# Expert rows scaled at the expert tile and summed in memory by adding DMAs, on one Trainium2 core

## What is computed

```python
def layer(x, w_qkv, b_qkv, w_out, b_out, w12, w3, gate_w):   # cut to what matters
    xn = layernorm(x)
    qkv = xn @ w_qkv + b_qkv                                 # windows of 128, stride 64, 16 heads
    attn = (softmax(q @ k.T / sqrt(16)) @ v)[:, :512] @ w_out + b_out
    top, idx = top_k(xn @ gate_w.T, 2)
    p = softmax(top)
    h = silu(xn @ w1[e]) * (xn @ w2[e])                      # for both experts e of a token
    ffn = sum(p[k] * (h[k] @ w3[idx[k]].T) for k in (0, 1))
    return x + attn + ffn
```

## Time and profile before

| | |
|---|---|
| median of 3 runs | 704.5 us (704.3 to 704.83) |
| the profiled execution: own time, span | 704.97 us, 703.2 us |
| mean granted TensorE clock | 0.981 |
| busy: TensorE, VectorE, ScalarE, GpSimd | 90%, 81%, 73%, 40% of the span |
| DMA | 92.62 MB, mean 132 GB/s |
| the chain that ended last, by engine | PE 65%, DVE 14%, ACT 10%, issue 7% |

### The profile page before, as it was taken

How to read it: one execution, slowest core, us unless ns; L and a number is a source line. 1 busy time by engine, 2 the same in 40 slices (tenths; PEclk the granted TensorE clock), 3 DMA queues, 4 the chain that set the end, 5 groups by cost and what they waited for, 6 DMA issues and landing times.

```text
span 703.2 us, 17940 instructions
## 1 busy us (share of the span) xinstructions
PE 630.0 (90%) x5914; PEld 509.7 (72%) x5915; DVE 567.5 (81%) x902; ACT 513.2 (73%) x882; POOL 281.5 (40%) x330
## 2 busy tenths in 40 slices
PE   0786785989999999999999999999999999999985
PEld 0554564765888888888888888888767676666663
DVE  4968899986888888888888888888587979788884
ACT  4554578396787787777877877777577788888885
POOL 3000274033344444444544544444201336666654
PEclk9998789899999999999999999999999999999999
DMA  9795478491111111111111111111178778885740
GB/s 299 263 257 193 110 251 305 121 314 48 53 52 52 60 52 52 59 48 57 53 52 60 52 53 60 52 52 54 38 192 242 180 246 209 262 228 159 207 141 31
DMA packets 66337, 92.62 MB, mean 132 GB/s; under 512 B 6432, under 2 KB 53408, under 8 KB 66272
## 3 DMA queue, kind: packets, MB, share of 16 engines
q1 hardware_dynamic: 57904, 70.56, 33.8%
q0 software_dynamic: 6816, 18.62, 7.9%
q10 hardware_dynamic: 1568, 2.76, 1.2%
HBM read 58.93 MB, written 32.83 MB: 130 GB/s over the span
## 4 chain that ended last, share of the span: by engine, by line
PE 65%; DVE 14%; ACT 10%; issue 7%; POOL 2%; DMA 1%; ACTq 0%; DVEq 0%; POOLq 0%
PE PS L1319 57%; PE PS L1570 4%; DVE SMALL L980 4%; ACT WORK L785 3%; PE PS L1548 2%; DVE XN L1138 2%; DVE WALL L974 2%; ACT QS L780 1%; DMA XN<-in_x 1%; DVE WORK L1049 1%; DVE WORK L1042 1%; ACT WORK L723 1%; DVE WALL L998 1%; ACT SIDE L792 1%; POOL OTS L595 1%
## 5 line engine op out<-in xcount | busy, mean ns | idle before, releaser
L367 DVE TENSOR_TENSOR WS<-WALL,WS 128x1024 fp32r<-128x1024 f32 x134 | 164.4, 1227 | 55.2 <-ACT WS L877 40.8
L1319 PE MATMUL PS<-WS,XTS 128*128 128x512 f32 x804 | 203.9, 402 | 0.0
L1319 PEld LDWEIGHTS PS<-WS,XTS 128*128 128x128 f32 x804 | 146.2, 189 | 30.5
L877 ACT ACTIVATE WS<-WALL 128x1024 fp32r x134 | 141.6, 1056 | 8.8 <-issue 0.3
L1319 PE MATMUL PS<-DOWN_HIGH,HTS 128*128 x568 | 115.9, 289 | 0.8 <-ACT HTS L892 0.8
L595 POOL TENSOR_TENSOR OTS<-SIDE,XN 128x256 f32<-128x256 f32 x30 | 22.8, 761 | 205.2 <-DVE XN L1138 138.5
L1319 PEld LDWEIGHTS PS<-DOWN_HIGH,HTS 128*128 128x128 f32 x568 | 90.9, 188 | 1.6 <-issue 1.5
L980 DVE TENSOR_REDUCE SMALL<-PS 128x8 f32<-128x1024 f32 x64 | 77.5, 1211 | 12.2 <-PE PS L1319 11.9
L785 ACT ACTIVATE WORK<-PS 128x512 f32<-128x512 f32 x128 | 69.4, 595 | 23.6 <-PE PS L1319 20.3
L667 POOL DMA_INDIRECT ys_scratch<-SIDE,SIDX x36 | 43.8, 1218 | 93.2 <-ACT SIDE L908 93.2
L663 POOL DMA_INDIRECT XS<-xn_scratch,GIDX x71 | 71.8, 1011 | 23.0 <-issue 21.3
(11 more groups left out here) (147 smaller groups left out, 1090.9 us busy)
## 6 DMA issues: line engine op xcount, KB each, us to landing
WALL<-in_wexp SPq DMA_DIRECT2D x28, 384.0 KB, 7.1
WALL<-ys_scratch SPq DMA_DIRECT2D x16, 512.0 KB, 7.2
parts_scratch<-WORK SPq DMA_DIRECT2D x32, 240.0 KB, 2.4
QS<-parts_scratch SPq DMA_DIRECT2D x16, 480.0 KB, 4.6
XN<-in_x SPq DMA_DIRECT2D x4, 1024.0 KB, 12.1
xn_scratch<-XN SPq DMA_DIRECT2D x4, 1024.0 KB, 7.3
WALL<-in_x SPq DMA_DIRECT2D x8, 512.0 KB, 5.9
KS<-parts_scratch SPq DMA_DIRECT2D x16, 240.0 KB, 4.1
```

The source lines that it names most:

```text
L367: eng.tensor_tensor(out=WS[:, 1 - k, half, 1], in0=weights, in1=WS[:, 1 - k, half, 0].bitcast(F32), op=ALU.subtract).then_inc(low_ready[ha ...
L877: act.activation(WS[:, 1 - k, half, 0], weights, ACT.Copy).then_inc(high_ready[half], 1)
L1319: return pe.matmul(o, a, b, start=start, stop=stop)
```

## The change

The rows of `xn_scratch` get two elements more: the share of the token's first choice and the difference of the second's to it. ScalarE stores them at batch 0, unit 5. A gather brings them along; GpSimd makes of them and of `KIND` (1 in slots of second choices) the share of each slot (`find_share`), and ScalarE's copy of a tile's result scales by it. `sum_scratch` replaces `ys_scratch`: one row for a token. SP copies `x` into it, GpSimd adds the attention rows of batches 0 and 1 (`keep`), and each scatter adds its rows, one scatter after the other. Behind the stage, `rest` loads one tensor, `own` is one add and is made for batches 2 to 7, `later`, `scale` and `combine` are gone, and batches 0 and 1 are copied from `sum_scratch` to the output.

```diff
-DUMP_ROW = 2 * B * L
+DUMP_ROW = B * L
+ROW = D + 2
...
-        XS = sb("XS", [P, 2, D])
+        XS = sb("XS", [P, 2, ROW])
...
-            yv = ys_dram[0:DUMP_ROW].rearrange("(k t p) d -> p t k d", k=2, p=P)
+            def copy_x(b):
+                r = slice(b * L, (b + 1) * L)
+                sp.dma_start(sum_dram[r], x[r]).then_inc(x_copied[b], 16)
 
             def rest(b):
-
                 t = slice(b * TB, (b + 1) * TB)
-                sp.dma_start(XR[:, t, :], xv[:, t, :]).then_inc(rest_in[b], 16)
-                for k in range(2):
-                    sp.dma_start(YG[:, t, k, :], yv[:, t, k, :]).then_inc(rest_in[b], 16)
...
+                sp.dma_start(XR[:, t, :], sv[:, t, :]).then_inc(rest_in[b], 16)
...
                 for half in range(2):
                     outs(b + 1, half)
                     backs(b + 1, (b + 1) % 2, half)
+                    if b == EXTRA and half == 0:
+                        sp.wait_ge(y_stored, 1)
+                        rest(EXTRA)
...
             load_experts(LATE, E)
-            keep(0)
-            load_tokens(2)
-            keep(1)
-            sp.wait_ge(rows_out, 16 * EXTRA)
-            sp.wait_ge(y_stored, 1)
+            load_tokens(EXTRA)
+            for b in range(B):
+                copy_x(b)
+            sp.wait_ge(phase_done, 3)
             sp.dma_start(KS[STK:DEEP, 1], KS[STK:DEEP, 0]).then_inc(hot_back, 16)
...
-                if b > OWN:
+                if b == EXTRA:
+                    for src in range(EXTRA):
+                        r = slice(src * L, (src + 1) * L)
+                        sp.dma_start(out[r], sum_dram[r]).then_inc(out_done, 16)
+                else:
                     send(b - 1)
...
+            def keep(b):
+
+                pool.wait_ge(r_free, (b + 1) * NWIN + 1)
+                pool.wait_ge(x_copied[b], 16)
+                t = slice(b * TB, (b + 1) * TB)
+                pool.dma_start(sum_dram[0:B * L].rearrange("(t p) d -> p t d", p=P)[:, t, :], XN[:, t, :],
+                               accum_op=ALU.add).then_inc(rows_out[b], 16)
...
             def own(b, n):
...
+                pool.wait_ge(rest_in[b], 16)
+                t = b * TB + n
+                pool.tensor_tensor(out=XR[:, t, :], in0=XR[:, t, :], in1=BOUT[:], op=ALU.add).then_inc(own_ready, 1)
...
             def scatter(j):
-                pool.indirect_dma_start(ys_dram, bass.IndirectOffsetOnAxis(SIDX[:, j:j + 1], 0),
-                                        YS[j % 2], None).then_inc(y_out[j % 2], 16)
+                if j:
+                    pool.wait_ge(y_out[1 - j % 2], 16 * ((j + 1) // 2))
+                else:
+                    for b in range(B):
+                        pool.wait_ge(x_copied[b], 16)
+                    for b in range(EXTRA):
+                        pool.wait_ge(rows_out[b], 16)
+                pool.indirect_dma_start(sum_dram, bass.IndirectOffsetOnAxis(SIDX[:, j:j + 1], 0),
+                                        YS[j % 2], None, compute_op=ALU.add).then_inc(y_out[j % 2], 16)
+
+            def find_share(j):
+                k = j % 2
+                pool.wait_ge(xs_in[k], 16 * (j // 2 + 1))
+                pool.tensor_scalar(out=SHARE[:, k:k + 1], in0=XS[:, k, D + 1:ROW], scalar1=KIND[:, j:j + 1],
+                                   scalar2=XS[:, k, D:D + 1], op0=ALU.mult, op1=ALU.add).then_inc(share_ready, 1)
+                pool.wait_ge(share_ready, j + 1)
...
                 pool.wait_ge(ys_ready, j + 2)
                 scatter(j)
+                if j + 2 < SLOT_TILES:
+                    find_share(j + 2)
...
-                    if b in LATER and u % 2 == 0:
-                        scale(LATER[b] * TB + u // 2, LATER[b], later_scaled)
-                    if b >= OWN and u % 2 == 1:
-                        scale(b * TB + u // 2, b, own_scaled)
...
+                    if b == 0 and u == 5:
+                        act.wait_ge(shares_made, 1)
+                        act.dma_start(xn_dram.rearrange("(t p) d -> p t d", p=P)[:, :, D:ROW], PW[:]
+                                      ).then_inc(shares_out, 16)
...
-                    act.activation(YS[k], bank(7)[:, 0:D], ACT.Copy).then_inc(ys_ready, 1)
+                    act.wait_ge(share_ready, j + 1)
+                    act.activation(YS[k], bank(7)[:, 0:D], ACT.Copy, scale=SHARE[:, k:k + 1]).then_inc(ys_ready, 1)
```

More of the change, by code:

```diff
@@ L331, in layer @@
         xt_full, xt_high, xt_free = sem("xt_full"), sem("xt_high"), sem("xt_free")
-        rows_out = sem("rows_out")
+        rows_out = [sem(f"rows_out{b}") for b in range(EXTRA)]
+        x_copied = [sem(f"x_copied{b}") for b in range(B)]
         high_ready = [sem("high_ready0"), sem("high_ready1")]
@@ L342, in layer @@
         rest_in = [sem(f"rest_in{b}") for b in range(B)]
-        rows_in = [sem(f"rows_in{b}") for b in range(EXTRA)]
         pool_step = sem("pool_step")
@@ L476, in send @@
                 sp.dma_start(ov[:, t, :], XN[:, t, :]).then_inc(out_done, 16)
-            def keep(b):
-                sp.wait_ge(r_free, (b + 1) * NWIN + 1)
-                t = slice(b * TB, (b + 1) * TB)
-                sp.dma_start(rv[:, t, :], XN[:, t, :]).then_inc(rows_out, 16)
             begin(0)
@@ L672, in _ @@
                 pool.wait_ge(parts_out[blk], PARTS_OUT[blk // 2] * (EXTRA + 1))
+            pool.wait_ge(shares_out, 16)
             gather(0)
@@ L676, in _ @@
             divide_halves(7)
+            find_share(0)
+            find_share(1)
             pool.wait_ge(xt_full, 1)
             gather(2)
+            for b in range(EXTRA):
+                keep(b)
             for j in range(SLOT_TILES):
@@ L689, in _ @@
                 for n in range(NWIN):
-                    if b in LATER:
-                        later(b, n)
-                    if b >= OWN:
-                        own(b, n)
+                    own(b, n)
                     if b * NWIN + n < B * NWIN - 1:
@@ L795, in sides @@
                 act.sem_inc(o_free, 1)
-            def scale(t, src, ready):
-                act.wait_ge(rest_in[src], 48)
-                for k in range(2):
-                    act.activation(YG[:, t, k, :], YG[:, t, k, :], ACT.Copy, scale=PW[:, k, t:t + 1]).then_inc(ready, 1)
             def part_of_places(i):
@@ L922, in _ @@
                     if j + 2 == EXACT_UP:
-                        act.wait_ge(rows_out, 16 * EXTRA)
+                        for b in range(EXTRA):
+                            act.wait_ge(rows_out[b], 16)
                     if split:
@@ L1177, in take_map @@
                 link(tt(MA, MA, MB, ALU.subtract))
-                link(ts(MB, hi, float(NT), float(B * L), ALU.is_gt, ALU.mult))
-                link(tt(MB, MA, MB, ALU.subtract))
+                link(ts(KIND[:], hi, float(NT), None, ALU.is_gt, ALU.bypass))
+                link(dve.scalar_tensor_tensor(out=MB, in0=KIND[:], scalar=-float(B * L), in1=MA, op0=ALU.mult,
+                                              op1=ALU.add))
                 link(dve.scalar_tensor_tensor(out=MAP[:, 1, :], in0=hi, scalar=0.0, in1=DUMP, op0=ALU.is_equal,
                                               op1=ALU.mult))
-                link(tt(MA, MA, MAP[:, 1, :], ALU.add))
+                link(tt(MA, MB, MAP[:, 1, :], ALU.add))
             def finish_map():
```

69 lines of the change are left out of this document (17 added, 52 removed).

## The result

The changed kernel took 714.25 us in the median of 4 runs (713.18 to 716.61), the kernel before 704.4 beside it (703.89 to 704.83): a ratio of 1.0145, 95% interval 1.0117 to 1.0172. The change is **9.9 us slower**, outside the predicted range and on the side of rival 2. All medians and ratios in this document are of fast executions; one of `adds_back`, 1551.62 us, is left out.

A forecast was written before the change was run, and what follows sets the result against it. TensorE was taken to bound the expert stage, with chains of waits in the attention batches. Terms +0.6 + 2.5 + 2.3 - 2.4 - 2.1 = +0.9 us on 704.5 gave 705.4 us, range 699.5 to 713.5.

The forecast's parts named there:

- rival 2: Expert stage entry: adds land at 178 to 182, TensorE waits 8 to 10 us; 711 to 713 us, chance 0.23.
- Entry: Entry into the expert stage: TensorE waits for gather 3 behind copies and adds, +2.5 us, bounds 0 and 10.
- Steady part: Expert stage: scatters one after another, landing in 3.2 us, and extra GpSimd work fit into the 4.84 us tile, 0.
- Batch 2: Entry into second attention part: load and bias add delay the first product, a cast slows, +2.3 us together.
- Batches 4 to 6: Dropped scalings and adds make these batches like batch 3, 0.8 us less each, -2.4 us, bounds -1.5 and -4.5.
- Last batch: Scaling leaves the ring of waits, about 0.7 us won in each of three windows, -2.1 us, bounds -1.2 and -3.2.
- ScalarE's issue: Batch 0, unit 5: ScalarE's DMA issue storing the shares is not hidden, +0.6 us, bounds 0.3 and 1.5.
- Rivals 3 and 4: rival 4, and expert stage: adding scatters landing after more than 4.8 us set the tile's time; near 740 us, chance 0.06.
- rival 4: Shares' store: 8-byte pieces above 0.18 us each delay the first gather; at 0.25 us, +18, 723 us; chance 0.04.

The follow-up runs named there:

- adds_back: The changed kernel with GpSimd's dropped adds put back in number, on the bias row and memory nobody reads, ScalarE untouched: 718.25 us, ratio 1.019.
- group 3: The changed kernel with its eight copies of x issued by SP ahead of batch 2's part stores: 716.39 us, ratio 1.0164.
- group 1: The changed kernel with dynamic_dma_scratch_size 3072 instead of 2048, nothing else: 712.46 us, ratio 1.0088.
- Groups 3 and 4: group 3, and the changed kernel without the two adding DMAs of batches 0 and 1 and the waits for them: 710.0 us, ratio 1.0057.
- group 8: The changed kernel with copies spread over batch 0, batch 0's add behind window 4's product, batch 2's load behind batch 3's first-half part stores: 703.36 us, ratio 0.998.
- group 5: The changed kernel with batch 2's load of the sum issued once the last scatter has landed, ahead of batch 3's stores and stack loads: 712.45 us, ratio 1.0114.
- group 6: The changed kernel with ScalarE's scalings, GpSimd's adds or both put back on unread data, then adds over one total, then old loads too: 717.09 to 722.54 us.

## Why the prediction was wrong, point by point

- *Entry, +2.5: measured +9.4. This is the step that failed.* I had the copies' end right (167.8), and gather 3 and scatter 0 as waiters; the adds were through at 176.2 and not at 172. I charged the adds 2.6 to 5.2 us together, by bytes at the rate of plain transfers. One alone takes 6.4 us to land (group 3), two beside copies 12.8 to 13.9 each (group 1), and in the change they ran one after the other, the second issued at 170.38, because GpSimd's queue had no room for both (group 1). The trace of the kernel before had rows that spoke against the price, and I did not read them. These are the landings of the two plain stores of the same rows (L481), 10.1 us beside the expert weights and 3.5 alone:

```profile
DMA to landing us min/median/max: 3.5/6.8/10.1
```

  Two terms were missing besides. Gather 2 beside the copies cost 2.3 us, and the lower clock behind the waits about 3.4. Groups 3 and 4 bound the shares: early copies save 6.9 of the 9.4, leaving out the adds 7.4. Together this is more than the whole, since an add is twice as slow beside the copies, and since either takes away the lower clock (granted 1.00 through both entries). This was rival 2, with the direction; the time it gave, 711 to 713, is just under the 714.25. It had not the queue's room. Whether the adds are slow beside the copies because small packets take turns with long pieces, as it had it, or because both share the memory, no run separates.
- *Steady part, 0: measured 0, and +0.7 in the last tile.* The term was right, by luck. I took 3.2 us for an adding scatter's landing and 4.0 as its upper bound, from plain ones; the first one took 4.73 and none here under 4.4. I bounded the 128x1 operation by a 128x256 one, 0.72; it took 1.67. The margin I gave as 1.6 us a tile was 0.1, and where the stage starts on time it is not always there (group 8: 1.8 us lost in the tiles ahead of the last). The Trainium skill (Collectives: The Full Stack, The bandwidth ceiling: the fold count and why AG ≠ RS ≠ AR) has a reducing transfer at about half the throughput because it reads two sources. 4.73 against 2.4 at best and 2.7 in the median agrees with it, and the 4.8 that I had worked out from it was the better estimate.
- *Batch 2, +2.3: measured +3.35, near +4.4 over the runs.* Mechanism right (group 5), size short. The load was issued 525.59 - 514.49 = 11.1 us into the part and landed in 5.1 us, both as estimated; the product came 1.73 later than before, just under the 1.9 to 3.0. What I left out is TensorE's lower clock behind the wait, 1.65 us. The 0.3 us for a slower cast did not come: the cast at 529.66 still took 0.33.
- *Batches 4 to 6, -2.4: measured -2.2* (and -0.1 in batch 3). The size was right, the reason only partly: neither scalings nor adds cost this by themselves (group 6); it came back with the adds over one total behind the scalings; such adds without the scalings were not tried.
- *Last batch, -2.1: measured -1.1.* Without its scaling ScalarE waits for GpSimd's product instead. That product was in the trace before: in the first window it ended at 676.67 + 0.73 = 677.40, so only 677.76 - 677.40 = 0.36 could be won there. I had compared with the end of TensorE's sums, 676.89, and not with the next wait. In the next two windows it ended 0.88 and 0.90 before the copy, yet no more came back there: the product waits for VectorE's reciprocals (5.03 us in the row above), which hang on the copies of the same round. The distances of the copies fell from 6.54 and 6.54 us (677.76, 684.30, 690.84) to 6.10 and 6.17 (687.23, 693.33, 699.50), so about 0.4 a window came back in all three.
- *ScalarE's issue, +0.6: measured 0.* ScalarE's timeline of the change around unit 5:

```profile
93.21 0.72 ACT L792 ACTIVATE XN<-XN,WALL 128x512 bf16<-128x512 bf16 x1
93.22 0.39 ACTq L809 DMA_DIRECT2D xn_scratch<-PW  x1
93.96 1.02 ACT L765 ACTIVATE QS<-PS 16x1024 bf16<-16x1024 bf16 x1
```

The issue lies beside the operation ahead of it. Before the change the same two stood at 94.92 and 95.66: the same distance.

- *Rivals 3 and 4.* The scatters did not set the tile's time in the change, by 0.1 us; in group 8 they did so for a few tiles. The 8-byte pieces landed after 11.5 us, and the first gather went at 143.25, not late: rival 4 was wrong. The Trainium skill (DMA: Bandwidth & Descriptors, Specifications) has writes under 512 B as read-modify-write; at 4096 pieces in 11.5 us nobody here waited for it.

## What to carry to other kernels

A DMA that adds is not a DMA that stores: price it at about twice the landing of a plain one (here 4.4 to 6.5 us against 2.7, and 6.4 against 3.5), more beside copies of the same memory, and look at what else GpSimd's queue must issue while it is under way. Put such transfers where nobody is behind them on that queue; the same copies and adds made the stage's entry 9.4 us longer in one place and 0.1 in another. Where a wait of TensorE is long enough, add what the lower clock behind it costs (here about 3.4 us at the entry, 1.65 in batch 2). When a step leaves a ring, find the wait that ends next among all engines, since the gain is at most the distance to that one, and less where that wait hangs on the same round.

## What the runs showed of the hardware that I had not expected

- Two adding DMAs of 512 KB (rows of 1 KB) did not fit together into GpSimd's queue with `dynamic_dma_scratch_size=2048`: the second held the engine 11.39 us. With 3072 it held it 0.16.
- An adding DMA of 512 KB landed in 5.8 to 6.5 us alone and in 11.6 to 12.6 beside copies within HBM, two at once there in 12.8 and 13.9 (the plain store of the kernel before in 3.5 alone); an adding scatter of 128 rows of 1 KB in 4.4 us at best, the plain one in 2.4.
- GpSimd's operation on 128x1 elements took 0.92 to 1.89 us, 1.67 in the mean, more than twice its 128x256 add of 0.72. In the change's expert stage the two short ones (178.10: 0.94, 508.69: 0.92) follow on a scatter's issue like the long ones, so the issue is not what makes it long; they are the two beside which VectorE does nothing, while every one of 1.47 us or more has some 1.2 us of VectorE's 128x1024 operation `WS<-WALL,WS` or as much of other VectorE work beside it. That VectorE makes it long was not tried.
- Eight copies of 512 KB within HBM took from 149.2 to 167.8 us, 7.7 to 14.2 each, behind expert weights; spread out, each landed in 4.3 to 6.9 us.
- Adding scatters kept the DMA engines busy for 34% of the steady part, plain ones for 16%, at 55 and 54 GB/s. The scatter's issue took GpSimd 1.7 us instead of 1.2.
